# Two bf16 transposes of row maxima widened to 128 columns by zero padding

## The chip, the cores and the metric

The kernel runs on one core of a Trainium2 chip. The metric is device time in microseconds (us) of one execution, the median of several runs. A core has a matrix engine (TensorE, in the rows PE; its weight loads are PEld), a vector engine (DVE), an activation engine (ACT), a general engine (POOL, also called GpSimd), and a queue engine (SP) that issues DMAs. Each walks its own list of instructions in order; semaphores tie the lists together.

## The reference, cut to what matters

Sixteen sequences of 128 tokens with 256 features go through four residual steps: attention over a context without weights (A), a mixture of experts (B), attention with weights and a causal mask (C), and a quantised feed-forward (D). The change touches the softmax of A and C.

```python
x = x + _L0_xattn_ref(_layernorm(x), ctx_512, ctx_512)         # A: 32 heads of 8
x = x + _L0_ffn_ref(_layernorm(x), ...)                        # B: 8 experts, 2 chosen, 1 shared
x = x + _L1_xattn_ref(_layernorm(x), ctx_512, Wq, Wkv, Wout)   # C: 16 heads of 16, causal
x = x + _L1_ffn_ref(_layernorm(x), w1, w2)                     # D: quantised inputs and weights
# in A and in C, for each head:
weights = jax.nn.softmax(scores, axis=-1)    # exp(score - row maximum) / sum
```

## The kernel before

Each of the 16 sequences is a tile t of 128 rows. A tile's work is cut into parts, named by stage and step (A1, A2.0, ..., D4), and an order written out by hand says, engine by engine, which part of which tile comes next; "A3/4" is part A3 of tile 4. The parts of up to four stages and several tiles are interleaved on each engine. TensorE's list also gives the bank of PSUM that a part writes; before the part's first matmul it waits until the bank's last reader is done (`fill`).

**The way of the row maxima.** Scores are computed twice. A2 (L613) multiplies queries by keys once with queries as rows, and DVE takes the negated maximum over the keys of each row (L1213), 32 heads a tile in A, 16 in C (C4, L735). POOL splits each maximum into two bf16 parts (L1089, L1090), so that A has 64 columns of maxima and C has 32. TensorE transposes them (A3, L620; C5, L742): the maxima are the weights that are loaded, and a bf16 identity of 128 columns is the operand that moves. ACT copies the result out of PSUM (L881, L885), SP sends it by DMA as two more rows of the queries, and the second product (A4, L628; C6, L750) then has the maximum already taken off, so that ACT can take exp from PSUM (L889).

**Shapes on TensorE.** The weights of most parts are 128 columns with 128 rows, or 96 to 98 rows (C2.1, C4, C6). A2 and A4 have 48 and 50 rows, two at a time in the two halves of the array. A5 (L640) and C7 (L759) have weights of 32 columns, four side by side. A3 has 64 columns, C5 has 32. A1, B1, C1, C9 and D1 all run through one helper, `turn` (L598): two transposes, in fp32 except D1's, which are bf16. A6 (L648), B5 (L685) and C8 (L767) are fp32 transposes, D3 (L798) bf16 ones. B2 to B4 (L661), B6 (L694), C2.0 (L715) and C10 (L777) are fp32 matmuls, D2 (L790) and D4 (L807) bf16 ones. A few parts in the list have filler matmuls ahead of them (L428, full shape), marked * below.

**The neighbours in TensorE's list**, the part before and the part after each transpose, by tile:

- A3: 0 A1, A2.1; 1 A4.3, A5.0*; 2 B3, B4; 3 B4, A5.0; 4 A6.1, B5.2; 5 A4.2, B2; 6 C7, B5.1; 7 A4.3, A1; 8 D1, C2.0; 9 C4.1, D1; 10 D1, C6.0; 11 B3, C2.0; 12 C9, C1; 13 D2, B2; 14 B6, D4; 15 A6.0, B3
- C5: 0 A2.1, A2.2; 1 A2.3, C9; 2 C2.1, A4.0; 3 A6.1, B5.1; 4 D4, C9; 5 A2.1, A5.1; 6 A4.0, D3; 7 B2, C1; 8 C1, A5.0; 9 A2.0, B6; 10 B3, B4; 11 A6.1, A2.0; 12 B4, B5.0; 13 B6, C7; 14 D4, C6.0*; 15 D2, D4

**Other things touched.** `ones` is a 128 by 128 tile of 1.0, used as the moving operand's partner in the sums over the weights of D at the start (S1, L580; S2, L589). `y2` is a pair of buffers that D4 writes (L1314, DVE). DVE's list begins with a few memsets (L1141 to L1145) and the bf16 copy of the identity (L1147), then takes the statistics of the first x as it lands (L1178).

Of the kernel before, what the change touches and what calls it, by code (L numbers as in the profile page):

```python
# [18 lines left out]
BF16 = mybir.dt.bfloat16  # L19
# [4 lines left out]
P = 128  # L24
D = 256
# [4 lines left out]
BANK = 512  # L30
# [4 lines left out]
H0 = KV0 * G0  # L35
J0 = KV0 // 2

H1, HD1 = 16, 16
# [224 lines left out]
def build(nc, a, out, TILES):  # L263
# [8 lines left out]
    with ExitStack() as ctx:  # L272
        def sb(name, shape, dt=F32):
            return ctx.enter_context(nc.sbuf_tensor(name, shape, dt))

        def sem(name):
            return ctx.enter_context(nc.semaphore(name))
# [3 lines left out]
        full = [sem(f"bank{i}_full") for i in range(BANKS)]  # L281
# [1 line left out]

        ident = sb("ident", [P, P])
        identb = sb("identb", [P, P], BF16)
        ones = sb("ones", [P, P])
        onesb = sb("onesb", [P, P], BF16)
        mask = sb("mask", [P, P], BF16)
        before = sb("before", [P, E, E])
# [18 lines left out]
        def two(name, shape, dt=F32):  # L308
            return [sb(f"{name}_{u}", shape, dt) for u in range(2)]
# [12 lines left out]
        QP = two("QP", [P, 2, 3, P], BF16)  # L322
        QA = two("QA", [P, H0 // 2, P], BF16)
        nmA = two("neg_maxA", [P, H0])
        nm2A = sb("neg_max2A", [P, 2, 2, H0 // 2], BF16)
        mTA = two("neg_maxT_A", [2 * H0, P], BF16)
        VA = two("VA", [P, KV0, SLOT])
        PA = sb("PA", [P, H0, P])
# [20 lines left out]
        KC = two("KC", [KM, H1, P], BF16)  # L349
        QC = two("QC", [KM, H1, P], BF16)  # L350
        nmC = two("neg_maxC", [P, H1])
        nm2C = sb("neg_max2C", [P, 2, H1], BF16)
        mTC = two("neg_maxT_C", [2 * H1, P], BF16)
        VC = two("VC", [P, H1, SLOT])
        PC = sb("PC", [P, H1, P])
# [10 lines left out]
        zbuf = sb("z", [P, 2, HF])  # L366
        w_abs1 = sb("w_abs1", [P, HF])
        y2 = two("y2", [P, D])
        gq_words, gT_words = sb("gq", [P, HF // 2]), sb("gT", [P, HF // 2])
        gq = gq_words[:].bitcast(BF16)  # L370
        gT = gT_words[:].bitcast(BF16).rearrange("p (k t) -> p k t", t=P)
# [6 lines left out]
        w_abs = [PC[:, 8:16, :].rearrange("p h t -> p (h t)"), w_abs1[:]]  # L378
# [18 lines left out]
        class Slot:  # L397
# [24 lines left out]
            def fill(self):  # L422
                for tile, p in uses[self.tile, self.part][2]:
                    _, name, per_tile, k = PARTS[p]
                    self.eng.wait_ge(S[name], tile * per_tile + k)
                ps, ready = self.view(self.part)
                for _ in range(FILLERS.get((self.part, self.tile), 0)):
                    nc.tensor.matmul(ps[:, 0:BANK], onesb[:], onesb[:].unsqueeze(1).broadcast_to([P, BANK // P, P]),  # L428
                                     start=True, stop=True)
                return ps, ready  # L430
# [29 lines left out]
        def walk(eng, engine, parts):  # L460
            for part, tile in PROGRAM[engine]:
                name, _, j = part.partition(".")
                parts[name](Slot(eng, part, tile), tile, tile % 2, *([int(j)] if j else []))
# [104 lines left out]
        def _(pe):  # L568
            mm, transpose = nc.tensor.matmul, nc.tensor.transpose

            def bf(ps):
                return ps[:].bitcast(BF16)
# [3 lines left out]
            def S1(s, t, u, j):  # L576
                ps, full = s.go_on("S1.0") if j else s.fill()
                pe.wait_ge(S["f1_abs"], j + 1)
                for b in range(2):
                    last = mm(ps[:, b * BANK:(b + 1) * BANK], ones[:], w_abs[j][:, b * BANK:(b + 1) * BANK],  # L580
                              start=(j == 0), stop=(j == 1))
                if j:
                    last.then_inc(full, 1)

            def S2(s, t, u, j):
                ps, full = s.go_on("S2.0") if j else s.fill()
                pe.wait_ge(S["f2_abs"], j + 1)
                for k in range(4):
                    last = mm(ps[:, 0:D], ones[:], w_abs[j][:, k * D:(k + 1) * D], start=(j == 0 and k == 0), stop=(j == 1 and k == 3))  # L589
                if j:  # L590
                    last.then_inc(full, 1)

# [24 lines left out]
            def A3(s, t, u):  # L617
                ps, full = s.fill()
                s.wait("nm2A", t)
                transpose(bf(ps)[0:2 * H0, 0:P], nm2A[:].rearrange("p c i h -> p (c i h)"), identb[:]).then_inc(full, 1)  # L620

            def A4(s, t, u, j):
                ps, full = s.fill()
# [115 lines left out]
            def C5(s, t, u):  # L739
                ps, full = s.fill()  # L740
                s.wait("nm2C", t)
                transpose(bf(ps)[0:2 * H1, 0:P], nm2C[:].rearrange("p i h -> p (i h)"), identb[:]).then_inc(full, 1)  # L742

            def C6(s, t, u, j):
                ps, full = s.fill()
# [55 lines left out]
            def D4(s, t, u):  # L801
# [4 lines left out]
                for k in range(FC):  # L806
                    last = mm(ps[:, 0:D], gT[:, k, :], f2q[:, k, :], start=(k == 0), stop=(k == FC - 1))  # L807
                last.then_inc(full, 1)

            pe.wait_ge(S["idents"], 1)  # L810
            walk(pe, "tensor", {"S1": S1, "S2": S2, "A1": A1, "A2": A2, "A3": A3, "A4": A4, "A5": A5, "A6": A6, "B1": B1, "B2": B2,
                                "B3": B3, "B4": B4, "B5": B5, "B6": B6, "C1": C1, "C2": C2, "C4": C4, "C5": C5, "C6": C6,
                                "C7": C7, "C8": C8, "C9": C9, "C10": C10, "D1": D1, "D2": D2, "D3": D3, "D4": D4})

# [323 lines left out]
        def _(dve):  # L1138
            v = nc.vector
            chain = Chain(dve, "dve")  # L1140
            v.memset(onesb[:], 1.0).then_inc(S["onesb"], 1)  # L1141
            for x in cT:
                v.memset(x[L:LK, :], 0.0)
            v.memset(w_kv[L:LK, :], 0.0).then_inc(S["pads"], 1)
            v.memset(ones[:], 1.0)  # L1145
            dve.wait_ge(pool_fill, 2)
            v.tensor_copy(identb[:], ident[:]).then_inc(S["idents"], 1)  # L1147

# [228 lines left out]
```

## Time and profile before

| | us |
|---|---|
| median of 3 runs | 573.54 (570.7 to 574.29) |
| profiled execution, its own time | 570.23 |
| its span in the profile | 568.4 |
| TensorE, matmuls busy | 502.9 (88%) |
| TensorE, weight loads busy | 321.2 (57%) |
| DVE busy | 373.9 (66%) |
| ACT busy | 362.2 (64%) |
| POOL busy | 283.9 (50%) |

The profiled execution is one execution with the profiler on; its time is close to the lowest of the runs, and 1.8 us of it lie outside the span. Busy times of TensorE count each matmul from its start to its modelled end, and the next one starts before that end, so they show when the engine has work, not how much faster it could be. The chain of work that ended last follows the last instruction back, at each step to what released it or to the instruction before it on its engine; its pieces run from the end of one piece to the end of the next, and add up to the span.

### The profile page before, as it was taken

To read this page: it belongs to the slowest core of one execution; us is meant where nothing else is said; L and a number is where in the kernel's file an instruction comes from. 1 tells how busy PE (TensorE), PEld (TensorE's weight loads), DVE (VectorE), ACT (ScalarE), POOL (GpSimd) and SP (SyncE) were. 2 spreads that over 40 slices of the span, in tenths; PEclk is the share of its full clock that TensorE was granted. 3 is DMA by queue.
4 is the path that set the end of the run, shared out by engine and by line. 5 is a ranking of instruction groups with operands and counts; after the bars stand their busy time and mean duration, and the time that the engine had idled before them with its cause. 6 is when DMAs were issued, how large, how long until landed. Compare 5 with 4: busy or idle time off the path is not lost.

```text
span 568.4 us, 10923 instructions
## 1 busy us (share of the span) xinstructions
PE 502.9 (88%) x3887; PEld 321.2 (57%) x3887; DVE 373.9 (66%) x816; ACT 362.2 (64%) x707; POOL 283.9 (50%) x535
## 2 busy tenths in 40 slices
PE   0078879999999999998999999999999999998784
PEld 0043435664666476755566656765575557676442
DVE  4545885574777747589767746797746845648654
ACT  1237553647556775789877576695679664576853
POOL 7359985444265363556443553545353443265321
PEclk9999999999999999999999999999999899999998
DMA  8955511312151221324211322143033110114000
GB/s 238 344 155 170 142 49 39 87 18 72 28 134 29 76 52 48 88 69 108 74 53 28 105 56 73 18 111 82 4 87 85 44 46 0 43 55 134 21 10 19
DMA packets 66445, 43.99 MB, mean 77 GB/s; under 512 B 36616, under 2 KB 61064, under 8 KB 66392
## 3 DMA queue, kind: packets, MB, share of 16 engines
q1 hardware_dynamic: 60064, 37.56, 25.1%
q10 hardware_dynamic: 6328, 5.73, 3.4%
q8 instruction: 32, 0.52, 0.4%
q14 instruction: 21, 0.17, 0.1%
HBM read 30.49 MB, written 12.39 MB: 75 GB/s over the span
## 4 chain that ended last, share of the span: by engine, by line
PE 70%; ACT 9%; DVE 6%; POOL 5%; issue 3%; ACTq 3%; DMA 2%; SPq 1%; POOLq 0%
PE banks L661 20%; PE banks L694 11%; PE banks L640 4%; PE banks L598 3%; PE banks L685 3%; PE banks L613 2%; PE banks L759 2%; PE banks L715 2%; PE banks L777 2%; PE banks L628 2%; PE banks L648 2%; PE banks L730 2%; PE banks L735 2%; ACT PC L889 2%; PE banks L807 2%
## 5 line engine op out<-in xcount | busy, mean ns | idle before, releaser
L1213 DVE TENSOR_REDUCE neg_maxA<-banks 128x8 f32<-128x1024 f32 x64 | 76.3, 1212 | 23.0 <-PE banks L613 22.9
L1117 POOL TENSOR_TENSOR vB<-vB,route_c 128x512 f32<-128x512 f32 x32 | 35.2, 1101 | 89.1 <-DVE vB L1272 88.9
L889 ACT ACTIVATE PA<-banks 128x1024 f32<-128x1024 f32 x64 | 63.9, 1031 | 11.7 <-PE banks L628 11.5
L913 ACT ACTIVATE tB<-banks,route_half 128x128 f32<-128x128 f32 x128 | 36.4, 368 | 49.5 <-PE banks L661 49.4
L694 PE MATMUL banks<-w2T,hTB 128*128 128x256 f32 x288 | 65.6, 382 | 1.0 <-ACT PC L889 0.9
L661 PE MATMUL banks<-w1T,xTB 128*128 128x512 f32 x128 | 61.1, 600 | 3.1 <-DVE vB L1265 3.1
L661 PE MATMUL banks<-w3T,xTB 128*128 128x512 f32 x128 | 60.1, 592 | 0.0
L694 PEld LDWEIGHTS banks<-w2T,hTB 128*128 128x128 f32 x288 | 53.7, 190 | 10.5 <-issue 2.0
L1233 DVE SCALAR_TENSOR_TENSOR tB<-tB,banks 128x512 f32<-128x512 f32 (+1 forms) x48 | 26.3, 548 | 28.8 <-ACT tB L913 28.6
L1213 DVE TENSOR_REDUCE neg_maxC<-banks 128x8 f32<-128x1024 f32 x32 | 38.5, 1214 | 7.5 <-PE banks L735 7.5
L1125 POOL TENSOR_SCALAR_AFFINE_SELECT PC<-PC 128x1024 f32<-128x1024 f32 x32 | 34.8, 1100 | 16.2 <-ACT PC L889 16.2
L661 PEld LDWEIGHTS banks<-w3T,xTB 128*128 128x128 f32 x128 | 24.3, 190 | 30.6 <-issue 30.6
L661 PEld LDWEIGHTS banks<-w1T,xTB 128*128 128x128 f32 x128 | 22.3, 190 | 23.0 <-issue 19.4
L889 ACT ACTIVATE PC<-banks 128x1024 f32<-128x1024 f32 x32 | 32.0, 1027 | 4.5 <-PE banks L750 4.3
L640 PE MATMUL banks<-PA,VA 128*32 128x512 f32 x256 | 32.1, 600 | 0.3 <-DVE neg_maxA L1213 0.3
L598 PE MATMUL banks<-ident,xnA 128*128 128x128 f32 x32 | 7.3, 312 | 25.2 <-ACT xnA L870 24.1
L613 PE MATMUL banks<-KA,QA 48*128 48x128 bf16 x512 | 23.8, 221 | 4.1 <-ACT PA L889 1.3
L926 ACT ACTIVATE hTB<-banks 128x512 f32<-128x512 f32 (+1 forms) x48 | 23.1, 502 | 6.4 <-PE banks L685 6.1
L1298 DVE SCALAR_TENSOR_TENSOR z<-banks,qscale,f_scale 128x1024 f32<-128x1024 f32 x16 | 20.4, 1278 | 9.0 <-PE banks L790 9.0
L628 PE MATMUL banks<-QA,KA 50*128 50x512 bf16 x128 | 22.8, 387 | 2.9 <-ACT PA L889 0.9
L613 PEld LDWEIGHTS banks<-KA,QA 48*128 48x128 bf16 x512 | 15.1, 95 | 17.9 <-issue 8.6
L685 PE MATMUL banks<-ident,vB 128*128 128x128 f32 x144 | 23.0, 278 | 1.8 <-ACT PC L889 1.2
(191 smaller groups left out, 1195.4 us busy)
## 6 DMA issues: line engine op xcount, KB each, us to landing
parts_qA<-QP SPq DMA_DIRECT2D x16, 192.0 KB, 2.5
QA<-parts_qA SPq DMA_DIRECT2D x32, 96.0 KB
parts_kC<-KPC SPq DMA_DIRECT2D x16, 192.0 KB, 2.1
KC<-parts_kC SPq DMA_DIRECT2D x16, 192.0 KB, 2.9
parts_qC<-QPC SPq DMA_DIRECT2D x16, 192.0 KB, 2.1
QC<-parts_qC SPq DMA_DIRECT2D x16, 192.0 KB, 2.9
x<-in_x SPq DMA_DIRECT2D x16, 128.0 KB, 7.4
QA<-parts_qA SPq DMA_DIRECT2D x32, 64.0 KB
```

The source lines that it names most:

```text
L613: last = mm(ps[:, c * BANK + g * P:c * BANK + (g + 1) * P], QA[u][rows, G0 * j + g, :], KA[rows, t // KCHUNK, j, t % KCHUNK * P:(t % KCHUN ...
L628: last = mm(ps[:, c * BANK:(c + 1) * BANK], KA[rows, t // KCHUNK, j, t % KCHUNK * P:(t % KCHUNK + 1) * P], QA[u][rows, G0 * j:G0 * (j + 1) ...
L640: last = mm(ps[SLOT * j:SLOT * (j + 1), :], VA[u][:, kv, :], PA[:, kv * G0:(kv + 1) * G0, :], start=True, stop=True)
L661: last = mm(ps[:, o:o + n], xTB[u][:, c, :], w[c], start=(c == 0), stop=(c == DC - 1))
L685: last = transpose(ps[:, i * P:(i + 1) * P], hB[:, (e0 + i) * HID:(e0 + i + 1) * HID], ident[:])
L694: last = mm(ps[:, 0:D], hTB[:, e, :], w_2[:, e, :], start=(e == 0), stop=(e == NE - 1))
L889: return op(dst[:, 8 * j:8 * (j + 1), :], ps[:].rearrange("p (h t) -> p h t", t=P), ACT.Exp, scale=scale).then_inc(S[name], 1)
L913: ins = op(tB[:, (e0 + i) * HID:(e0 + i + 1) * HID], ps[:, i * HID:(i + 1) * HID], ACT.Tanh, scale=rt["half"][:, e0 + i:e0 + i + 1])
L1117: g.tensor_tensor(hB[:, sl].rearrange("p (e h) -> p e h", e=4), vB[:, sl].rearrange("p (e h) -> p e h", e=4), rt["c"][:, e0:e0 + 4].unsque ...
L1125: g.affine_select(out=p, in_=p, compare_op=ALU.is_ge, fill=0.0, base=0, pattern=[[0, 8], [1, P]], channel_multiplier=-1).then_inc(S["PC_ca ...
L1213: v.tensor_reduce(dst[:, 8 * j:8 * (j + 1)], ps[:].rearrange("p (h t) -> p h t", t=P), FREE, ALU.max, negate=True).then_inc(S[name], 1)
L1233: return v.scalar_tensor_tensor(out=uB[:, lo:lo + n], in0=tB[:, lo:lo + n], scalar=1.0, in1=ps[:, 0:n], op0=ALU.add, op1=ALU.mult)
```

## The change

The maxima get buffers of 128 columns, zero beyond the 64 (A) or 32 (C) that are used; `nm2A` and `nm2C` become views of their first columns. Both transposes load all 128 columns and write all 128 partitions of the result; ACT still copies out the first 64 or 32. The zeros are written once, by two memsets on DVE at the start. `ones` is no tile of its own any more but the first half of `y2[0]`. The order of parts on every engine stays.

```diff
-        ones = sb("ones", [P, P])
...
-        nm2A = sb("neg_max2A", [P, 2, 2, H0 // 2], BF16)
+        wide2A, wide2C = sb("neg_max2A", [P, P], BF16), sb("neg_max2C", [P, P], BF16)
+        nm2A = wide2A[:, 0:2 * H0].rearrange("p (c i h) -> p c i h", c=2, i=2)
+        nm2C = wide2C[:, 0:2 * H1].rearrange("p (i h) -> p i h", i=2)
...
-        nm2C = sb("neg_max2C", [P, 2, H1], BF16)
...
         y2 = two("y2", [P, D])
+        ones = y2[0][:, 0:P]
...
-                    last = mm(ps[:, b * BANK:(b + 1) * BANK], ones[:], w_abs[j][:, b * BANK:(b + 1) * BANK],
+                    last = mm(ps[:, b * BANK:(b + 1) * BANK], ones, w_abs[j][:, b * BANK:(b + 1) * BANK],
...
-                    last = mm(ps[:, 0:D], ones[:], w_abs[j][:, k * D:(k + 1) * D], start=(j == 0 and k == 0), stop=(j == 1 and k == 3))
+                    last = mm(ps[:, 0:D], ones, w_abs[j][:, k * D:(k + 1) * D], start=(j == 0 and k == 0), stop=(j == 1 and k == 3))
...
             def A3(s, t, u):
                 ps, full = s.fill()
                 s.wait("nm2A", t)
-                transpose(bf(ps)[0:2 * H0, 0:P], nm2A[:].rearrange("p c i h -> p (c i h)"), identb[:]).then_inc(full, 1)
+                transpose(bf(ps)[:, 0:P], wide2A[:], identb[:]).then_inc(full, 1)
...
             def C5(s, t, u):
                 ps, full = s.fill()
                 s.wait("nm2C", t)
-                transpose(bf(ps)[0:2 * H1, 0:P], nm2C[:].rearrange("p i h -> p (i h)"), identb[:]).then_inc(full, 1)
+                transpose(bf(ps)[:, 0:P], wide2C[:], identb[:]).then_inc(full, 1)
...
             for x in cT:
                 v.memset(x[L:LK, :], 0.0)
+            v.memset(wide2A[:, 2 * H0:], 0.0)
+            v.memset(wide2C[:, 2 * H1:], 0.0)
             v.memset(w_kv[L:LK, :], 0.0).then_inc(S["pads"], 1)
-            v.memset(ones[:], 1.0)
+            v.memset(ones, 1.0)
```

## Rows read from the trace of the kernel before

**Rows 1.** The page: the span, and the chain that ended last, by engine.
```profile
span 568.4 us, 10923 instructions
...
PE 70%; ACT 9%; DVE 6%; POOL 5%; issue 3%; ACTq 3%; DMA 2%; SPq 1%; POOLq 0%
```

**Rows 2.** Busy time by stretch: PE, PEld, DVE, ACT, POOL, granted clock, DMA share, GB/s.
```profile
120.00:500.00 380.00, 369.68 (x2890) 241.15 (x2891) 261.89 (x588) 263.82 (x532) 178.68 (x336) 1.00 0.24 61
```

**Rows 3.** Lines L620 and L742: durations in ns (min/median/max), first and last start, shapes.
```profile
L620 PEld LDWEIGHTS banks<-identb,neg_max2A x16: 106/106/107, 42.6 to 449.1; 128*64 128x64 bf16 x16
L620 PE MATMUL banks<-identb,neg_max2A x16: 216/243/244, 42.6 to 449.1; 128*64 128x128 bf16 x16
...
L742 PEld LDWEIGHTS banks<-identb,neg_max2C x16: 92/92/93, 122.7 to 532.3; 128*32 128x32 bf16 x16
L742 PE MATMUL banks<-identb,neg_max2C x16: 216/230/230, 122.7 to 532.3; 128*32 128x128 bf16 x16
```

**Rows 4.** Groups by line and shape: weight loads; busy us, mean ns | idle before.
```profile
L694 PEld LDWEIGHTS banks<-w2T,hTB 128*128 128x128 f32 x288 | 53.7, 190 | 10.5 <-issue 2.0 <-ACT PC L889 1.1 <-ACT hTB L926 0.6
...
L807 PEld LDWEIGHTS banks<-f2q,gT 128*128 128x128 bf16 x128 | 11.8, 98 | 5.7 <-ACT gT L973 2.9 <-issue 0.8 <-ACT PA L889 0.2
```

**Rows 5.** The chain around A3/4: start us, us, what.
```profile
120.86 0.37 PE banks L598 x2
121.22 0.44 PE banks L648 x4
121.66 0.17 PE banks L620
121.83 0.59 PE banks L685 x4
```

**Rows 6.** The chain around D1/8, a bf16 transpose of 128 columns.
```profile
394.28 0.11 PE banks L598 x2
394.39 0.44 PE banks L648 x4
```

**Rows 7.** The chain: equal work behind different neighbours, seven places.
```profile
231.81 0.87 PE banks L807 x8
...
305.53 0.89 PE banks L715 x8
...
327.00 1.09 PE banks L715 x8
...
372.09 0.22 PE banks L598 x2
...
382.64 3.44 PE banks L661 x8
...
408.68 3.63 PE banks L661 x8
...
425.68 0.98 PE banks L807 x8
```

**Rows 8.** The chain: C5/8 with A5/11 behind it, and A5/12 behind C4/9.
```profile
357.02 0.16 PE banks L742
357.18 1.72 PE banks L640 x16
...
391.40 1.85 PE banks L640 x16
```

**Rows 9.** The chain: first and last of 22 pieces of L620 and L742.
```profile
95.23 0.17 PE banks L620
...
505.78 0.16 PE banks L742
```

**Rows 10.** The start: DVE's timeline [idle before], and one piece of the chain.
```profile
2.06 0.17 DVE L1145 MEMSET ones<- 128x128 f32 x1
...
2.96 0.43 DVE L1178 BATCH_NORM_STATS2 statsA<-x 128x6 f32<-128x256 f32 x1 [0.66 <-DMA x<-in_x]
...
15.70 5.64 ACTq L833
```

## The prediction

> **What bounds the kernel now.** I read the page first, then the busy time by stretch, then the chain of work that ended last, and last the lines of the two transposes that the change touches. The page gives a span of 568.4 us and puts 70% of the chain on TensorE, 9% on ACT, 6% on DVE [rows 1]. By stretch it is sharper: from 120 to 500 us TensorE is busy 369.68 of 380 us, 97%, against 262 for DVE and 264 for ACT, at a granted clock of 1.00, which is the 2.4 GHz level [rows 2]. Of the 32 transposes, 25 lie in that stretch (A3/0 to A3/3 come before it, C5/13 to C5/15 after it). There, time taken out of TensorE's own stream is mostly time taken out of the kernel; before 120 and after 500 us TensorE waits for others more often.
>
> **What the two transposes cost today.** Each is one weight load and one matmul. By line, A3 (L620) loads 64 columns in 106 ns and its matmul takes 243 ns; C5 (L742) loads 32 columns in 92 ns and takes 230 ns [rows 3]. Sixteen of each are 7.6 us of matmul, but matmuls overlap, so durations are the wrong price. The chain has the right one, since its pieces run from end to end. An A3 is a piece of 0.17 us, a C5 one of 0.16 us [rows 5, 8]. The same kind of transpose with 128 columns of the same type is on the chain too: D1's two stand as 0.11 us, 0.055 us each [rows 6].
>
> The second half of the price lies in the work that follows. After A3/4 four fp32 transposes (B5.2, L685) take 0.59 us; after D1 four of the same shape (A6, L648) take 0.44 [rows 5, 6]. After C5/10 the eight matmuls of B4 take 3.63 us, while another B4 that follows full-width work takes 3.44; C2.0's eight take 1.09 after A3/11 and 0.89 elsewhere; D4's eight in bf16 take 0.98 after A3/14 and 0.87 elsewhere [rows 7]. So the follower pays 0.15 us (fp32 transposes), 0.19 to 0.20 (fp32 matmuls, taken as 0.195) or 0.11 (bf16).
>
> What the pieces with the surcharge share is the shape of the work before them. Not only A3 and C5 cause it: two fp32 transposes right after A2 (48 rows) take 0.37 us, two after D4 (128 by 128) take 0.22 [rows 5, 7]. And where C5 (32 columns) is followed by A5, whose weights are also 32 columns, A5's 16 matmuls take 1.72 us, whereas after a full-width neighbour they take 1.85 [rows 8]. I read this as: going from one shape of work in the array to another costs TensorE, and staying in a shape costs nothing. The shapes here are full (128 columns, more than 64 rows), A2/A4 (48 and 50 rows), A5/C7 and today's C5 (32 columns), and A3 (64 columns, alone).
>
> **The change, part by part.**
>
> *The widening.* Both transposes become full. With a full neighbour ahead, the own piece falls from 0.17 to 0.055 (saves 0.115 for A3) and from 0.16 to 0.055 (0.105 for C5). With a full neighbour behind, the follower's surcharge goes. With A2/A4 on a side, that side keeps its price. With A5/C7 behind, an A3 keeps that side's price and a C5 loses the shared shape: 1.85 less 1.72, 0.13 us, is added. The neighbours are those of the list in the section on the kernel; 22 of the 32 transposes have their piece on the chain, 11 of each kind, the first at 95.23, the last at 505.78 us [rows 9]. Over these 22:
>
> - A3 with full work on both sides, tiles 4, 8, 10, 11, 13, 14, 15: 7 x 0.115 + 0.15 (4) + 4 x 0.195 (8, 11, 13, 15) + 2 x 0.11 (10, 14) = 1.955.
> - A3/12: its follower waits for something else, so the own piece alone, 0.115.
> - C5 with full work on both sides, tiles 4, 7, 10, 12: 4 x 0.105 + 3 x 0.15 + 0.195 = 1.065.
> - Full work ahead alone: A3/3 0.115, C5/2 0.105, C5/8 and C5/13 each 0.105 - 0.13, together 0.17.
> - Full work behind alone: A3/6, A3/7, C5/1 at 0.15, C5/6 at 0.11, C5/9 at 0.195: 0.755.
> - C5/0 stands between two A2: 0.
>
> Sum: 1.955 + 0.115 + 1.065 + 0.17 + 0.755 = 4.06 us. The other ten are hidden by a wait of TensorE or stand beside a chain that runs over ACT, DVE or POOL; I count them at nothing. By the same prices they would give some 1 us of TensorE time. If the cover went, that is what they could add.
>
> *The weight load.* A 128-column bf16 load is in the trace: 98 ns for D4's [rows 4], against today's 106 and 92 [rows 3]. So the load doesn't grow, and D1's 0.055 us a transpose shows that it is hidden. The bound above is the 190 ns of an fp32 load of 128 columns [rows 4]; I take 98, since type and width are the same. The Trainium skill (TensorE: Matmul & The Clock Gate, section LDWEIGHTS) speaks against the change here: it gives a load as columns divided by 1.2, so 53 ns for A3, 27 for C5, 107 for both after it. By it 16 x 54 + 16 x 80 = 2.1 us of loading would be added (an estimate from that page), and the sum would be 4.06 - 2.1 = 2.0 us if none of it were hidden. The trace disagrees with it: 106, 92 and 98 ns don't rise with the columns.
>
> *Zeros, copies, POOL.* The padding is written once, by two DVE memsets at the start; one of 128 columns takes 0.17 us [rows 10], so they are at most 0.34. DVE then idles 0.66 us for the first x [rows 10], which hides them, and the chain of the start runs over ACT's queue, one piece of which alone is 5.64 us [rows 10]. Without that cover they would cost 0.34. POOL's and ACT's work on the maxima keeps its shapes (the copies still read 64 and 32 rows).
>
> *ones in y2.* The same memset into another buffer, with the same shape for the sums. y2 is first written far later (D4/0), behind the sums in TensorE's order. No wait is added: 0.
>
> **What of the 4.06 us arrives.** Between 70% (TensorE's share of the chain, rows 1) and 97% (its busy share where these pieces lie, rows 2); I take the middle, 84%: 3.4 us. The rest is lost where the chain goes over to an exp on ACT or a maximum on DVE that wouldn't have started earlier. The profiled execution would come to 570.23 - 3.4 = 566.8 us. It lies 3.3 us below the median of the runs, 573.54, and even below their lowest, 570.7; the same step from the median gives 570.1.
>
> **The rivals.**
> - *The surcharge isn't the width's* (7%). It could belong to these instructions for another reason, such as the wait each begins with. For it: no A3 or C5 of full width has run. Against it: D1's transposes wait too and take 0.055 us. Then nothing is saved and the three C5 before A5 or C7 (tiles 5, 8, 13) may add 3 x 0.13: 573.5 to 573.9 us.
> - *Another engine takes over* (10%). ACT and DVE have 264 and 262 us of work in a stretch of 380, but in bursts. If TensorE only reaches the next exp or maximum sooner, 0.3 to 2 us remain: 571.5 to 573.2. For it: the 30% of the chain that isn't TensorE. Against it: TensorE's idle time there is 10 us in all.
> - *The others count as well* (8%): 4.06 + 1 = 5.1 us, 568.4.
> - *Slower: the wider load stands in the open* (3%). If a full-width load of these tiles behaved like the fp32 one, 190 ns, and the switching stayed, it would cost 16 x 84 + 16 x 98 ns = 2.9 us, and with the three C5 3.3: 576.8 us. It decides as soon as the load no longer runs beside the matmul before it. Against it: rows 4 and 6. The Trainium skill's rule on loads, weighed above, is the same mechanism with the switching gone: by it 573.54 - 2.0 = 571.5 us.
>
> **How the numbers follow.** My forecast, 2 to 4.1 us less, has 70%; the rivals have 7, 10, 8 and 3%; 2% is left for what I don't see. The likeliest time is 570.1 us. The range runs from the profiled execution less the whole sum, 570.23 - 4.06 = 566.2, taken as 566, to the highest run of before with nothing gained, 574. A measurement here can tell about 1% from no change, 5.7 us. No case gains that much by its mechanism; the runs shown spread over 3.6 us, so a favourable set could show it: faster 0.10, same 0.87, slower 0.03.
>
> **What would show it.** After the change the loads of both lines should show 128 columns and 97 to 100 ns; their pieces of the chain 0.06 us where full work stands ahead; B5.2 after A3/4 0.44, B4 after C5/10 3.44, C2.0 after A3/11 0.89 us; A5 after C5/8 1.85. TensorE's busy time should hardly move, since it counts durations that overlap. I am wrong if the pieces stay at 0.16 and more, if the loads grow, or if the pieces shrink as said and the span stays, which would mean that other engines hold the stretch from 120 to 500 us.

## The result, and the profile after

The changed kernel takes 571.05 us, the median of 22 runs (565.66 to 572.89), against 574.65 us for the kernel before in 22 runs beside it. The ratio is 0.9939 with a 95% interval of 0.9915 to 0.9962: 0.61% or 3.5 us less.

The profiled execution of the changed kernel nevertheless has a longer span than that of the kernel before, 570.3 against 568.4 us [rows 1]. The busy times by stretch say why, first the kernel before, then the changed kernel, with the columns of [rows 2] (PE, PEld, DVE, ACT, POOL, granted clock, DMA share, GB/s):

```profile
30.00:120.00 90.00, 79.79 (x520) 45.04 (x521) 57.48 (x103) 48.40 (x104) 60.76 (x102) 1.00 0.37 98
```

```profile
30.00:120.00 90.00, 80.37 (x476) 44.34 (x477) 53.88 (x99) 46.49 (x97) 58.42 (x98) 0.92 0.38 98
120.00:500.00 380.00, 367.74 (x2904) 240.79 (x2915) 264.55 (x592) 264.29 (x537) 179.21 (x335) 1.00 0.24 61
```

In the changed kernel's execution the granted clock was 0.92 from 30 to 120 us, because it stood at half speed (1.2 GHz) in three places there, within 50 to 54, 74 to 81 and 84 to 88 us. In the profiled execution of the kernel before it was 1.00 over the same stretch. A3/4 therefore begins at 127.15 us instead of 121.66 [rows 5], 5.5 us late, and the end is only 1.9 us late: 3.6 us were made up behind it. Whether the fall of the clock belongs to the change is a question for the experiments below; where the two profiles are to be compared, it has to be done inside the stretch from 120 to 500 us, at a clock of 1.00.

Line numbers after the change are one higher on TensorE's lines: A3 is L621, C5 L743, `turn` L599, A5 L641, A6 L649, the experts L662, B5 L686, B6 L695, C2.0 L716, D4 L808. The weight loads of the two transposes by line (durations in ns, min/median/max; compare [rows 3]):

```profile
L621 PEld LDWEIGHTS banks<-identb,neg_max2A x16: 95/97/105, 43.2 to 450.8; 128*128 128x128 bf16 x16
...
L743 PEld LDWEIGHTS banks<-identb,neg_max2C x16: 95/98/100, 127.9 to 533.8; 128*128 128x128 bf16 x16
```

And the chain of the work that ended last, at the places of [rows 5], [rows 7] and [rows 8] and a few more (start us, us, what):

```profile
127.15 0.06 PE banks L621
127.21 0.44 PE banks L686 x4
...
179.64 0.16 PE banks L621
...
331.12 0.95 PE banks L716 x8
...
361.05 1.85 PE banks L641 x16
...
412.11 0.06 PE banks L743
412.17 3.49 PE banks L662 x8
...
428.86 0.06 PE banks L621
428.91 0.87 PE banks L808 x8
...
451.04 0.06 PE banks L621
...
495.06 0.06 PE banks L743
```

A3/4 is a piece of 0.06 us where it was 0.17, and the four transposes behind it take 0.44 where they took 0.59 [rows 5]. C5/10 is 0.06 where C5/8 was 0.16 [rows 8], and B4 behind it takes 3.49 where it took 3.63; D4 behind A3/14 takes 0.87 where it took 0.98 [rows 7]. A3/6, with C7 (32 columns) ahead of it, still costs 0.16 us (179.64). A5 behind C5/8 has gone up from 1.72 to 1.85 us [rows 8]: this is the shape that was shared and now is not. C2.0 behind A3/11 takes 0.95 us where it took 1.09; the forecast had 0.89.

The start holds the two new memsets (DVE's timeline, idle before in brackets; compare [rows 10]):

```profile
1.49 0.09 DVE L1145 MEMSET neg_max2A<- 128x32 uint32 x1
1.53 0.10 DVE L1146 MEMSET neg_max2C<- 128x48 uint32 x1
...
2.92 0.43 DVE L1181 BATCH_NORM_STATS2 statsA<-x 128x6 f32<-128x256 f32 x1 [0.33 <-DMA x<-in_x]
```

They take 0.09 and 0.10 us, and DVE's wait for the first x shrinks from 0.66 to 0.33 us; its first statistics begin at 2.92 us instead of 2.96.

### The profile page after: what moved, and what is told of

It reads as the page before. It is cut to its first block, busy times and chain, and to the rows that moved or that the text cites. A ratio compares the mean times of both kernels' runs of the same rounds, so it can differ in the third digit from the quotient of the medians.

```text
span 570.3 us, 10910 instructions
## 1 busy us (share of the span) xinstructions
PE 503.4 (88%) x3872; PEld 322.1 (56%) x3887; DVE 373.9 (66%) x818; ACT 362.2 (64%) x707; POOL 284.2 (50%) x535
## 4 chain that ended last, share of the span: by engine, by line
PE 71%; ACT 12%; DVE 5%; issue 3%; ACTq 3%; POOL 2%; DMA 2%; SPq 0%; POOLq 0%
PE banks L662 21%; PE banks L695 11%; PE banks L641 5%; PE banks L599 3%; PE banks L686 3%; ACT PC L890 3%; PE banks L614 2%; PE banks L649 2%; PE banks L629 2%; PE banks L716 2%; PE banks L760 2%; PE banks L778 2%; PE banks L731 2%; PE banks L736 2%; DMA QC<-neg_maxT_C 2%
## 5 line engine op out<-in xcount | busy, mean ns | idle before, releaser
L695 PE MATMUL banks<-w2T,hTB 128*128 128x256 f32 x288 | 65.6, 382 | 1.0 <-ACT PC L890 0.9
L662 PE MATMUL banks<-w1T,xTB 128*128 128x512 f32 x128 | 62.8, 614 | 3.2 <-DVE vB L1268 3.2
L662 PE MATMUL banks<-w3T,xTB 128*128 128x512 f32 x128 | 61.4, 602 | 0.0
L695 PEld LDWEIGHTS banks<-w2T,hTB 128*128 128x128 f32 x288 | 53.8, 190 | 10.5 <-issue 2.0
L662 PEld LDWEIGHTS banks<-w3T,xTB 128*128 128x128 f32 x128 | 24.9, 195 | 31.7 <-issue 31.7
L662 PEld LDWEIGHTS banks<-w1T,xTB 128*128 128x128 f32 x128 | 22.9, 194 | 24.3 <-issue 20.3
L641 PE MATMUL banks<-PA,VA 128*32 128x512 f32 x256 | 32.2, 603 | 0.3 <-DVE neg_maxA L1216 0.3
L599 PE MATMUL banks<-ident,xnA 128*128 128x128 f32 x32 | 7.5, 319 | 24.2 <-ACT xnA L871 23.0
L686 PE MATMUL banks<-ident,vB 128*128 128x128 f32 x144 | 23.3, 281 | 1.8 <-ACT PC L890 1.2
```

What stands on the lines that cost most here:

```text
L641: last = mm(ps[SLOT * j:SLOT * (j + 1), :], VA[u][:, kv, :], PA[:, kv * G0:(kv + 1) * G0, :], start=True, stop=True)
L662: last = mm(ps[:, o:o + n], xTB[u][:, c, :], w[c], start=(c == 0), stop=(c == DC - 1))
L686: last = transpose(ps[:, i * P:(i + 1) * P], hB[:, (e0 + i) * HID:(e0 + i + 1) * HID], ident[:])
L695: last = mm(ps[:, 0:D], hTB[:, e, :], w_2[:, e, :], start=(e == 0), stop=(e == NE - 1))
```

## The experiments

The theory: TensorE pays when the shape of the work in the array changes, once at the transpose and once at what follows, and the change takes such changes of shape away. The rivals: the gain comes from something else in the change; another engine takes over; or it is the number of columns itself that matters, by the load.

**The kernel before against itself.** The measure of the noise, and of the clock.

> The kernel before against itself. Ratio 1.000 within its interval, which gives the noise of the comparisons. It also gives the granted clock of more executions of before. If the early fall of the clock that the profile of the changed kernel shows (0.92 from 30 to 120 us, where the profile of before has 1.00) belongs to the change, these executions stay near 0.993; if it is the chance of an execution, most lie at 0.981 to 0.988 like those of the changed kernel.

Measured: ratio 0.9997, interval 0.9964 to 1.0031. The lists of runs give the mean granted clock of each execution. Of the 35 executions of the kernel before that this comparison shares, 5 had a mean granted clock of 0.99 or more and 28 one of 0.985 or less; of the changed kernel's 22, it was 2 and 17. A low clock is thus common to both kernels, and the profile of before had happened on an execution with a high one. A mean doesn't say where the clock fell, but the profile of this run has one fall at the place of the changed kernel's second (and none at its other two):

```profile
74.00:81.00 7.00, 7.00 (x26) 2.99 (x26) 2.98 (x6) 0.48 (x2) 5.20 (x5) 0.59 0.30 88
...
120.00:500.00 380.00, 367.86 (x2877) 238.94 (x2887) 263.07 (x588) 263.55 (x533) 178.12 (x334) 1.00 0.24 61
```

It ran at 1.00 from 120 to 500 us without a break, whereas the first profile of before fell to 0.50 for 3.4 us at 440.8. So it is the better partner for a comparison inside that stretch. The chain of this execution, at A3/4 and at C5/12:

```profile
124.98 0.17 PE banks L620
...
496.23 0.16 PE banks L742
```

From the start of A3/4's piece to the start of C5/12's are 496.23 - 124.98 = 371.25 us here, and 495.06 - 127.15 = 367.91 us in the changed kernel: 3.34 us less. The terms of the prediction's sum that lie between these two points are 4.06 less 0.115 (A3/3), 0.255 (C5/12) and -0.025 (C5/13), so 3.72 us. A second execution of the changed kernel, profiled for the last comparison below and also at 1.00 throughout this stretch, needs 367.75 us for it: 3.50 less.

**Each transpose alone.** The changed kernel with one of the two narrow again.

```diff
-                transpose(bf(ps)[:, 0:P], wide2C[:], identb[:]).then_inc(full, 1)
+                transpose(bf(ps)[0:2 * H1, 0:P], wide2C[:, 0:2 * H1], identb[:]).then_inc(full, 1)
```

> The changed kernel with C5 at 32 columns again (its own transpose reads and writes the first 32; buffers and memsets stay). My theory, that a change of shape on TensorE is what costs: A3's terms of the sum stay, 1.955 + 0.115 + 0.115 + 0.30 = 2.49 us, of which 84% arrive, so 2.1 us less than before (ratio 0.996); the pieces of C5 on the chain are 0.16 us again and those of A3 0.06. Rival, that other engines hold the kernel and the gain of the changed kernel comes from somewhere else (the buffers, the start): no relation to the terms, ratio 1.000 or 0.994 like the whole change.

Measured: ratio 0.9966 (0.9934 to 0.9998), 2.0 us less than before, where 2.1 was expected. On the chain A3/4 is 0.06 us and C5/1 0.16; from A3/4 to C5/12 are 369.46 us, 1.79 less than the kernel before again.

```diff
-                transpose(bf(ps)[:, 0:P], wide2A[:], identb[:]).then_inc(full, 1)
+                transpose(bf(ps)[0:2 * H0, 0:P], wide2A[:, 0:2 * H0], identb[:]).then_inc(full, 1)
```

> The changed kernel with A3 at 64 columns again. My theory: C5's terms stay, 1.065 + 0.105 - 0.05 + 0.455 = 1.58 us, of which 84% arrive, so 1.3 us less than before (ratio 0.998); together with the run that widens A3 alone this should come to the whole change's 3.5 us. Rival: the two don't add up, since another engine takes over once TensorE is ahead (then each alone gives nearly the whole 3.5 us), or neither gives anything alone.

Measured: ratio 0.9949 (0.9915 to 0.9984), 2.9 us less where 1.3 was expected; the expected 0.998 is still inside the interval. From A3/4 to C5/12 are 369.27 us, 1.98 less. So A3 gave less in the stretch than its terms (1.79 of 2.37 us) and C5 more (1.98 of 1.35 us); together 3.77, against 3.34 for both at once. Both are needed for the whole gain, and neither gives it alone, which is against the rival that another engine takes over at once. That the halves add to 0.43 us more than the whole has a place on the chain: 0.49 us between A3/14 and A3/15 come with either half, and again only once with both (shown under "What arrives" below). Another part of the difference between the halves arises between 207 and 233 us, where a DMA of maxima and ACT stand on the chain, and there two executions of the same kernel before differ by 0.2 us as well. How the gain divides between the two transposes is settled no closer than that.

**Wider, but not full.** A3 at its 64 columns, C5 padded from 32 to 64.

```diff
-                transpose(bf(ps)[:, 0:P], wide2C[:], identb[:]).then_inc(full, 1)
+                transpose(bf(ps)[0:64, 0:P], wide2C[:, 0:64], identb[:]).then_inc(full, 1)
```

(with A3 as in the run before this one)

> Neither transpose is full: A3 has its 64 columns, C5 is padded from 32 to 64. Theory by shape: nothing is gained, since C5 still changes the shape on both sides, and the three C5 ahead of A5 and C7 lose the shape they shared, 3 x 0.13, with 0.01 us more for each piece (0.17 instead of 0.16): 0 to 0.5 us more than before, ratio 1.000 to 1.001. Rival, that more columns are cheaper in themselves: some of C5's 1.3 us is gained, ratio 0.998 to 0.999.

Measured: ratio 1.0024 (0.9992 to 1.0057). The chain has C5/8 as

```profile
361.67 0.17 PE banks L743
361.84 1.85 PE banks L641 x16
...
413.49 3.63 PE banks L662 x8
```

The piece is 0.17 us, A5 behind it has gone from 1.72 to 1.85, and B4 behind C5/10 pays its 3.63 as before. From A3/4 to C5/12 are 371.44 us, 0.19 more than the kernel before again. Padding by itself gains nothing; it loses the shape that C5 shared with A5. This run also has all else of the change (the wide buffers, the two memsets, `ones` in `y2`), and nothing comes of that: the rival that the gain comes from something else in the change falls here.

**Ninety-six columns.** This tells the shape from the load.

```diff
-                transpose(bf(ps)[:, 0:P], wide2A[:], identb[:]).then_inc(full, 1)
+                transpose(bf(ps)[0:96, 0:P], wide2A[:, 0:96], identb[:]).then_inc(full, 1)
...
-                transpose(bf(ps)[:, 0:P], wide2C[:], identb[:]).then_inc(full, 1)
+                transpose(bf(ps)[0:96, 0:P], wide2C[:, 0:96], identb[:]).then_inc(full, 1)
```

> The changed kernel with both transposes at 96 columns instead of 128. Theory by shape: 96 rows already behave as full in this kernel (C4's matmuls of 96 rows follow full work without a surcharge), so 96 columns should as well, and the ratio is that of the changed kernel, 0.994; the pieces are 0.06 to 0.07 us. Rival, that only a full load of 128 columns gets the fast path: the load takes more than 98 ns, the pieces stay between 0.10 and 0.17 us, and the time goes back by part or all of the gain (0.997 to 1.000).

Measured: ratio 0.9934 (0.9894 to 0.9975), that of the changed kernel. By line the load has become slower, and the chain shows where that counts:

```profile
L621 PEld LDWEIGHTS banks<-identb,neg_max2A x16: 119/123/153, 43.0 to 450.4; 128*96 128x96 bf16 x16
```

```profile
125.79 0.06 PE banks L621
125.84 0.44 PE banks L686 x4
126.29 0.33 PE banks L614 x8
126.62 0.19 PE banks L743
...
410.50 0.06 PE banks L743
410.56 3.49 PE banks L662 x8
```

The load takes 123 ns instead of 97. Behind full work (A3/4, C5/10) the piece is still 0.06 us, so the load is hidden there; only behind work of another shape (C5/0 behind A2) is it in the open, 0.19 instead of 0.16 us. So the gain is that of the shape, and a load that is 25 ns slower takes nothing from it that the time shows.

**The price by itself.** Thirty-two more transposes, ahead of each B6 and C10, with 32 or with 128 columns.

```diff
                 s.wait("hTB", t, 3)
+                transpose(bf(ps)[0:32, 0:P], identb[:, 0:32], identb[:])
                 for e in range(NE):
...
                 s.wait("oTC", t)
+                transpose(bf(ps)[0:32, 0:P], identb[:, 0:32], identb[:])
                 for c in range(DC):
```

> The changed kernel with 32 more transposes on TensorE: one of the identity's first 32 columns ahead of the matmuls of each B6 and each C10, into the bank that these then overwrite; it waits for nothing that they don't wait for. This measures the price by itself. Theory by shape: each is a piece of 0.16 us and adds 0.195 to the fp32 matmuls behind it, 32 x 0.355 = 11.4 us of TensorE, of which 84% arrive: 9.5 us more than the changed kernel, ratio to before about 1.010. Rival, that a transpose costs its own time alone: 32 x 0.055 = 1.8 us, the same as the next run.

> The same 32 more transposes, with all 128 columns of the identity. Theory by shape: 0.055 us each and nothing behind them, 1.8 us of TensorE, 1.5 us more than the changed kernel, ratio to before about 0.996. Rival, that the price is one of instructions and waits and not of the shape: as much as with 32 columns.

Measured: with 32 columns 1.0047 (1.0016 to 1.0079), with 128 columns 0.9927 (0.9895 to 0.9959). The difference is 1.2%, 6.9 us, or 0.22 us for each of the 32. Part of it is the clock: only 1 of the 12 executions with narrow ones had a mean clock of 0.99 or more, and 3 of the 11 with full ones that the ratio uses. At the same clock the difference is some 5.1 us, 0.16 us each (the table below). The chain at B6/2, first with 32 and then with 128 columns:

```profile
123.59 0.16 PE banks L694
123.75 4.08 PE banks L696 x18
```

```profile
127.89 0.06 PE banks L694
127.95 3.94 PE banks L696 x18
```

At this place the narrow transpose costs 0.10 us more itself and 0.14 us more in the 18 matmuls behind it, 0.24 us in all. The direction and the price by piece are those of the theory. Both ratios came out lower than expected (1.010 and 0.996): 32 narrow ones added 1.1% to the changed kernel's 0.9939 instead of 1.6%, and 32 full ones added nothing that can be seen in the ratio instead of 0.26%. At the same clock the full ones add 1.1 us to the changed kernel where 1.5 was expected, and the narrow ones 6.2 where 9.5 was (2.5 and -2.6 us against -3.7 in the table below, measured in two comparisons). The follower's price of 0.195 us was too high (0.14 at B6/2), and B6 and C10 begin with a wait for a copy on ACT at some tiles, beside which such a transpose may be hidden.

**Fillers in the idle time ahead of the clock's fall.** The profile of the changed kernel suggested it. TensorE's longest single wait ahead of the second fall (engine, line, waited for: us in total, times, longest) is, besides the first parts of the kernel,

```profile
PE banks L662 <- DVE vB L1268: 3.2, 1, 3.2
```

It is the wait of B4/0, right behind A3/2, and the clock falls in its last microsecond. The edit is one word in the list of fillers:

```diff
-    A2.0/1:7 A4.0/0:9 A5.0/0:6 C6.0/14:10 C6.0/15:4 C9/14:4 D3/13:7 D1/15:12 D2/15:3 D3/14:9
+    A2.0/1:7 A4.0/0:9 A5.0/0:6 A3/2:14 C6.0/14:10 C6.0/15:4 C9/14:4 D3/13:7 D1/15:12 D2/15:3 D3/14:9
```

> The changed kernel with 14 filler matmuls ahead of A3/2, where TensorE otherwise idles 3.2 us at 71.8 us right behind it. If that idle time is what lets the clock fall at 74 to 81 and 84 to 88 us in the profile of the changed kernel (10.2 us at half the clock), the clock stays at 1.00 there, and up to 5 us come back; as TensorE isn't the bound throughout that stretch, I expect 2 to 4 us less than the changed kernel, ratio to before 0.987 to 0.991. Rival: the fall comes from other idle times as well (2.1 us ahead of A3/1) or A4.0/2, which waits for A3/2's DMA, comes later: 0 or up to 3 us more than the changed kernel.

Measured: ratio 0.9897 (0.9866 to 0.9927), inside the expected 0.987 to 0.991. The stretch from 74 to 81 us, first in the changed kernel, then with the fillers, with the piece of the chain for B4/0 in each:

```profile
74.00:81.00 7.00, 5.97 (x7) 2.52 (x8) 3.83 (x9) 0.00 (x0) 5.44 (x6) 0.51 0.33 89
```

```profile
75.03 6.68 PE banks L662 x8
```

```profile
74.00:81.00 7.00, 5.48 (x43) 2.57 (x42) 5.80 (x8) 3.75 (x10) 6.09 (x7) 1.00 0.34 89
```

```profile
73.09 3.71 PE banks L662 x8
```

With the clock at 1.00 the eight matmuls of B4/0 take 3.71 us instead of 6.68, and ACT, which waits for them, has work in the stretch. A3/2 itself comes later by the fillers, and nothing on the chain waits for it. These two profiles alone don't show that the fillers did it: in the first profile of the kernel before TensorE idles there too, 3.1 us and without fillers, and the clock stays at 1.00 (B4/0 takes 3.71 us at 73.46). What the fillers do has to be read from how often the clock stays up.

Then the same fillers in the kernel before, the changed kernel again and the changed kernel with fillers again, side by side:

> The kernel before with the same 14 filler matmuls ahead of A3/2, and both transposes narrow as they were. If the fillers' gain has nothing to do with the widening, it is the same here: about 2.4 us (the step from 0.994 of the changed kernel to 0.990 with fillers), ratio 0.996, and the executions with a granted clock of 0.984 and less become fewer. Rival: the fillers only help the changed kernel; then the ratio is 1.000.

> The changed kernel once more, beside the two with fillers on one chip. Ratio 0.994 within its interval; with the run before it this says whether the two edits add up.

> The changed kernel with the 14 fillers ahead of A3/2 once more. If the edits add up, its ratio is that of the changed kernel times that of the kernel before with fillers, 0.994 x 0.996 = 0.990; if the first comparison flattered it, 0.992 to 0.994.

Measured: fillers in the kernel before 0.9976 (0.9942 to 1.0010); the changed kernel again 0.9944 (0.9910 to 0.9977); the changed kernel with fillers again 0.9878 (0.9839 to 0.9917). Of the executions with the fillers in the changed kernel, 11 of 18 had a granted clock of 0.99 or more, and with the fillers in the kernel before 8 of 12; without them, 7 of the 23 executions of before in this comparison, 1 of the 12 of the changed kernel in it and 2 of its first 22. So with the fillers more executions keep a high clock, in both kernels. The gain on the kernel before can't be told from none by the times alone. The product of the two edits, 0.9944 x 0.9976 = 0.9920, lies inside the interval of the first comparison with both edits and just outside that of the second, so the ratios leave open whether they add up or help each other; the expectation of 0.990 lies within both. The changed kernel with the fillers is the fastest kernel of this study, 5.9 and 7.0 us below the kernel before in the two comparisons.

**All runs at the same clock.** How many executions have a low clock differs from one set of the same kernel to the next (of the kernel before, 28 of 35 had 0.985 or less in one comparison and 14 of 23 in another), and it moves the ratios. An estimate that takes it out: in each of the three comparisons, one straight line of an execution's time on its mean granted clock, with one slope for all kernels in it. The three slopes are 4.7, 4.8 and 5.1 us for 0.01 of clock. What is left between a kernel and the kernel before, in us, with a 95% interval:

| kernel | by the ratio | at the same clock |
|---|---|---|
| A3 alone full | -2.0 | -2.4 ± 0.6 |
| C5 alone full | -2.9 | -2.2 ± 0.6 |
| 96 columns | -3.8 | -3.5 ± 0.6 |
| A3 64, C5 64 columns | +1.4 | -0.2 ± 0.6 |
| change and 32 narrow ones | +2.7 | +2.5 ± 0.5 |
| change and 32 full ones | -4.2 | -2.6 ± 0.6 |
| before again | -0.2 | +0.2 ± 0.6 |
| change again | -3.2 | -3.7 ± 0.5 |
| change and fillers | -5.9, -7.0 | -3.8 ± 0.6, -4.7 ± 0.7 |
| before and fillers | -1.4 | -0.2 ± 0.5 |

The order of the kernels is that of the theory, and the change by itself stands at 3.7 us. The fillers give nothing to the kernel before at the same clock and 0.1 to 1.0 us to the changed one, so their gain comes mostly by the clock.

## Why the prediction was right, point by point

The forecast was 3.4 us less, 570.1 us, by the end of changes of shape on TensorE. Measured were 3.5 us less.

**The bound.** The gain arrived where the prediction put it: 3.34 us between A3/4 and C5/12, where TensorE is busy 367.74 of 380 us after the change, 369.68 before [rows 2]. Its busy time hardly moved, as said. Not all of the 3.34 us comes from the terms, though; see "What arrives".

**The own piece.** Predicted 0.055 us behind full work, measured 0.06; predicted unchanged behind A2, A4 and C7, measured 0.16. Right. At A3/12 the saved 0.11 us didn't arrive: the piece called "issue" behind it, time in which the engine waited for nothing that the profile shows, grew from 0.01 to 0.13 us (374.77 before, 378.66 after). The prediction had said that this follower waits for something else, and counted 0.115 all the same; the runs show 0.

**The follower.** Predicted 0.44 us for B5.2 and 0.87 for D4 (0.98 less 0.11), measured 0.44 and 0.87. The term for fp32 matmuls was too large: 0.195 us each, measured 0.14 (3.63 to 3.49, 1.09 to 0.95 [rows 7]). It stands six times in the sum (A3/8, 11, 13, 15, C5/9, 10), so the sum was some 6 x 0.055 = 0.33 us too large. The step that failed is the choice of the cheap neighbour. I took B4 and C2.0 behind fp32 transposes (3.44 and 0.89), while behind a full bf16 transpose they take 3.49 and 0.95. The chain of the kernel before had the right price too, in an expert part behind C4's eight bf16 matmuls:

```profile
221.68 0.45 PE banks L735 x8
222.13 3.49 PE banks L661 x8
```

C2.0 behind D3 (bf16) takes 0.95 there as well (381.59). So the 0.05 us go with bf16 work ahead, not with a transpose that is short or stands alone. A possible reason is that an fp32 load of 190 ns [rows 4] hides less well behind bf16 work; no run tests this by itself.

**The loss of the shared shape.** Predicted 1.85 us for A5 behind C5/8, measured 1.85. Right, and the run with 64 columns shows the loss without the gain. At C5/13 it can't be read: the chain leaves TensorE behind it after the change.

**The weight load.** Predicted 98 ns and hidden, measured 97 and 98, and hidden. The rival of a load in the open fell. The run with 96 columns shows that the load could be 25 ns slower without a loss that the time shows.

**What arrives.** I took 84%. Inside the stretch 3.34 of 3.72 us arrived, 90%. That it came so close is in part luck, because 0.49 of the 3.34 us belong to no term. They arise between A3/14 and A3/15. The kernel before again has there

```profile
429.06 0.17 PE banks L620
...
451.95 0.17 PE banks L620
```

so 22.89 us, and the changed kernel 451.04 - 428.86 = 22.18. That is 0.71 us less, where the terms have 0.225. With A3 alone full it is 22.18, with C5 alone 22.40, where the terms have 0.225 and nothing; with 64 columns 23.14. In all of them the chain goes over to ACT in this place; from there it goes on over two maxima on DVE in the kernel before (from 442.95) and with 64 columns, and over TensorE in the changed kernel (from 442.79) and with either half. Why either half is enough for that no run shows.

Without the 0.49, 2.85 us of the terms arrived, 77% of the 3.72, or 84% once the follower is mended (3.72 - 0.33 = 3.39). The largest other loss is between A3/7 and C5/6, where 0.33 us came of 0.715; in the second profile of the changed kernel it is 0.63, so that executions differ there by as much. The forecast's number came out by a sum that was too large, a share near the truth, and a gain that I hadn't foreseen.

**Start and ones.** Predicted hidden, measured hidden: 0.33 of DVE's 0.66 us wait went into the memsets and what lies around them.

**The rivals.** That the surcharge isn't the width's fell with the narrow and full extra transposes (0.16 to 0.22 us apart each, with the same waits). That another engine takes over fell as a whole with the two halves, each of which gave part of the gain; between A3/14 and A3/15 alone it holds, since there one half gives as much over its terms as both. That the other ten count in full (5.1 us) isn't what the time shows. By the prediction's own prices and its list of neighbours they come to some 1.6 us rather than 1, so this rival stood at 5.7 us, further off still. One of them, C5/14, does stand on the chain of the kernel before, as a 23rd piece of 0.23 us at 532.33 between two waits; it takes 0.23 us in the second profile of the changed kernel too, so counting it at nothing was right.

**What I didn't foresee.** The clock. I had read the granted clock of 1.00 of one profile as the kernel's own, while most executions of both kernels lose some microseconds to a lower clock, in the profiled ones mostly in the start. It touched neither the forecast's mechanism nor its sign, since both kernels lose it. But the profile of the changed kernel would have misled a reader who compares the two spans, and how many executions of a run had a low clock moved the differences by up to 1.6 us where no fillers were added (the table above).

## What to carry to other kernels

On TensorE, price a small instruction by what its shape does to its neighbours, read from pieces of the chain of the same work behind different neighbours, and not by its duration. Here a narrow transpose among full-width matmuls cost several times the 0.06 us of a full one; zeros that bring it to the neighbours' shape were cheaper, and where the neighbour is narrow too, the narrow form is the right one. Take the cheap neighbour of the same type as the one that will stand there. Before two profiles are compared, lay the granted clock of each stretch side by side, and compare inside stretches where both have the same; where runs differ in their mean clock, compare times at the same clock.

## What the runs showed of the hardware

- A change of shape cost about 0.10 us at the transpose that enters (0.16 to 0.17 against 0.06 us) and 0.11 to 0.15 us at what follows (0.98 to 0.87, 3.63 to 3.49, 0.59 to 0.44); a transpose of 96 columns beside work of 128 showed no price (0.06 us, 3.49 behind it). The Trainium skill (TensorEngine Tiling (Array Packing), Key Properties) says that changing the tiling mode drains the array, without a figure. The trace agrees in that a change costs time; that the cost is a drain no run shows.
- Eight fp32 matmuls took 3.44 us behind full fp32 work, 3.49 behind full bf16 work and 3.63 behind a transpose of 32 or 64 columns.
- Loads of bf16 weights took 92 ns for 32 columns, 106 for 64, 123 for 96, and 97 for 128. The step down at 128 is what the Trainium skill (TensorE: Matmul & The Clock Gate, Weight-path perf modes) describes as the fast weight load, which needs 128 weights of a type other than fp32; the trace agrees in that 128 columns load faster than 96, and fp32 loads of 128 columns ahead of matmuls take 190 ns [rows 4]. The Trainium skill's rule (the same page, LDWEIGHTS) that a load takes its columns divided by 1.2 would give an estimate of 27, 53, 80 and 107 ns; the measured ones differ from it.
- At half the granted clock (1.2 GHz) eight fp32 matmuls of 512 columns took 6.68 us, at the full 2.4 GHz 3.71 us. TensorE had been idle right before the fall (3.2 us in all); in another execution, of the kernel before, it was idle 3.1 us at the same place and the clock stayed at 1.00. With 14 fillers in that idle time 11 of 18 executions of the changed kernel had a mean clock of 0.99 or more, without them 3 of 34.
